# The second layer's experts run between the third and the fourth sequence of attention instead of after it, and the closing gate and residual run inside the fourth sequence's head pairs

## The reference, cut to what matters

```
x  = x + s * g                                  # end of the first layer: "x2"
xn = layernorm(x)
s  = attention(xn)     # 16 heads of 64, rotary, causal, 1024 x 1024 per sequence, output projection Wo: "y"
g  = silu(moe(xn))     # 8 experts, each token goes to 2 of them, weighted; moe(xn) is the sum "z"
x  = x + s * g         # the result
```

## Time and profile before

| | us |
|---|---|
| median of 3 runs | 2559.09 (2556.2 to 2560.73) |
| the profiled execution | 2560.09, its span 2557.7 |
| attention, first to last matmul | 825.6 to 2109.8 |
| experts, first to last matmul | 2115.0 to 2515.0 |
| closing run | 2515.0 to 2557.7 |

### The profile page before, as it was taken

One profiled execution on the slowest core, in us unless ns is written; L12 is line 12 of the kernel. 1 busy time (PEld: TensorE's weight loads), 2 busy tenths in 40 slices (PEclk: granted clock), 3 DMA queues, 4 the chain that ended last, 5 costly groups with the idle time before them and its releaser, 6 DMA issues. The chain is left out here.

```text
span 2557.7 us, 45455 instructions
## 1 busy us (share of the span) xinstructions
PE 2421.2 (95%) x14584; PEld 1698.3 (66%) x14585; DVE 1328.0 (52%) x3699; ACT 1104.5 (43%) x2581; POOL 553.9 (22%) x510
## 2 busy tenths in 40 slices
PE   6999998999976899999999999999999999999993
PEld 5555555666645566666666666666666668999992
DVE  6666341222227866666666666666666653333334
ACT  3211111111115566666666666666666652222222
POOL 3002001444436233332111111111111101111113
PEclk9999998999988999999999999999999999999997
DMA  6013103975446233332111221112221217667696
GB/s 211 17 49 115 49 17 107 271 212 160 115 98 218 77 97 91 97 94 74 42 41 41 52 64 39 35 41 58 67 58 43 58 44 254 236 238 242 236 342 225
DMA packets 145366, 295.74 MB, mean 116 GB/s; under 512 B 16768, under 2 KB 102288, under 8 KB 134896
## 3 DMA queue, kind: packets, MB, share of 16 engines
q1 hardware_dynamic: 124320, 251.59, 31.1%
q0 software_dynamic: 20944, 42.94, 6.3%
HBM read 193.80 MB, written 67.12 MB: 102 GB/s over the span
## 5 line engine op out<-in xcount | busy, mean ns | idle before, releaser
L1463 ACT ACTIVATE at_p<-at_p,at_nmax 128x640 f32<-128x640 f32 (+7 forms) x512 | 392.6, 768 | 179.5 <-DVE at_nmax L1635 173.5
L1498 POOL TENSOR_TENSOR kept_big<-kept_xg 128x1024 f32<-128x1024 f32 x64 | 150.9, 2357 | 985.0 <-DVE kept_xg L1655 985.0
L1470 ACT ACTIVATE at_pT<-at_ps 128x512 f32<-128x512 f32 (+1 forms) x640 | 311.4, 574 | 104.8 <-PE at_ps L1418 104.8
L1635 DVE CUSTOM_DVE_ANT_0 at_p<-at_ps,atk_mask 128x512 f32<-128x512 f32 (+3 forms) x512 | 281.8, 585 | 138.2 <-PE at_ps L1410 134.9
L1418 PEld LDWEIGHTS at_ps<-kept_ident,at_p 128*128 128x128 f32 x2304 | 256.8, 141 | 106.5 <-issue 62.6
L1418 PE MATMUL at_ps<-kept_ident,at_p 128*128 128x128 f32 x2304 | 302.8, 277 | 7.0 <-ACT at_p L1463 6.4
L1410 PE MATMUL at_ps<-kept_big 64*128 64x512 f32 (+3 forms) x1536 | 296.9, 505 | 5.8 <-POOL kept_big L1498 3.3
L1432 PE MATMUL at_ps<-at_pT,at_v 128*64 128x256 f32 (+1 forms) x2560 | 270.2, 362 | 1.2 <-issue 1.2
L1670 DVE SCALAR_TENSOR_TENSOR kept_big<-at_ps,at_inv,kept_big 128x256 f32<-128x256 f32 x512 | 214.0, 475 | 82.0 <-issue 61.5
L1432 PEld LDWEIGHTS at_ps<-at_pT,at_v 128*64 128x64 f32 x2560 | 173.5, 137 | 115.1 <-issue 34.8
L1395 PE MATMUL at_ps<-atk_h,atk_w 128*128 128x512 f32 x512 | 238.0, 598 | 6.6 <-SPq L1257 6.6
(11 more groups left out here) (236 smaller groups left out, 3347.2 us busy)
## 6 DMA issues: line engine op xcount, KB each, us to landing
moe_w<-in_w_w SPq DMA_DIRECT2D x53, 1028.0 KB
kept_xg<-kept_xg SPq DMA_DIRECT2D x256, 128.0 KB
atk_first_w<-in_w_w SPq DMA_DIRECT2D x18, 1028.0 KB
atk_w<-in_w_qkv SPq DMA_DIRECT2D x32, 384.0 KB, 3.1
slot_in<-kept_big SPq DMA_DIRECT2D x9, 1032.0 KB
kept_big<-in_w_eg SPq DMA_DIRECT2D x16, 512.0 KB
kept_big<-in_w_eu SPq DMA_DIRECT2D x16, 512.0 KB
kept_big<-in_w_ed SPq DMA_DIRECT2D x16, 512.0 KB
```

The source lines that it names most:

```text
L1463: act.activation(buf, buf, ACT.Exp, bias=nmax[:, unit:unit + 1], scale=-1.0, accum_out=rsum[:, unit:unit + 1]).then_inc(exp_done, 1)
L1470: act.activation(dst, ring[RING_BANK[part][ev]][:, 0:(i1 - i0) * P].rearrange("p (k c) -> p k c", c=P), ACT.Copy).then_inc(t_read, 1)
L1498: pool.tensor_tensor(out=qkT[x][:, :].rearrange("p (m t) -> p m t", m=2)[:, :, half * CH:(half + 1) * CH], in0=raw[half][:, :].rearrange(" ...
L1635: ins = dve.tensor_tensor_reduce(out=p[unit % LAG][:, at:to], in0=ring[RING_BANK[part]["S", ((t, c), e), ahead]][:, 0:to - at], in1=mask[: ...
```

## The change

`attention` is called twice: for sequences 0 to 2 with the routing and the scatter (`scatter` true), then `moe`, then for sequence 3 alone with `scatter` false. The first call loads, in its last pairs, the projection weights, output weights and normalized input that sequence 3 starts with, and stores sequence 2's y from SBUF at its end. `moe` ends with its last tile; its output rows, their indices and their semaphores now belong to a scope that outlives it.

The closing run is cut into eight groups of 512 tokens and one is worked on in each pair of sequence 3, in the memory of the experts' second weights (`close`, two sets of four buffers of 128x1024). In pair g: SyncE loads both z tables, x2 and y of group g (no y for groups 6 and 7, which are sequence 3 itself), between the output weights and the swaps; GpSimd adds the two z (`begin`); ScalarE takes Exp of minus that, ahead of E6.0; GpSimd adds 1 (`plus`); VectorE takes the reciprocal, ahead of W2.0; in the next pair GpSimd multiplies (`finish`: z times the reciprocal is Silu of z; times y; plus x2), and SyncE stores. For groups 6 and 7 GpSimd makes only the gate, and VectorE multiplies y by it and adds x2 in the last pair, behind the adds of each W. In place of the one Silu there are Exp, plus one, reciprocal and a multiply.

```diff
+CLOSE_EXP, CLOSE_INVERT = ("E", (6, 0), 0), ("W", (2, 0), 0)
...
+        WHOLE = NCH - NCH // B
+        close = [[d.moe_w2[:, (4 * q + k) * TC * C:(4 * q + k + 1) * TC * C] for k in range(4)] for q in range(2)]
...
-                def pair(it, u, load_w, load_wo, half_free=lambda half: None):
+                def pair(it, u, load_w, load_wo, half_free=lambda half: None, then=lambda: None):
                     sp.wait_ge(w_ps, it * 4 + ONE)
                     sp.dma_start(wo[1 - u][:, :], load_wo).then_inc(wo_in[1 - u], 16)
+                    then()
                     for half in range(2):
                         swap(it + 1, half)
...
+                def close_load(g):
+                    q = g % 2
+                    if g >= 2:
+                        sp.wait_ge(close_out[q], 16 * (g // 2) + ONE)
+                    for k in range(TOP):
+                        sp.dma_start(view(close[q][k], g), piece_rows(d.z2, g, k)).then_inc(close_in[q], 16)
+                    sp.dma_start(view(close[q][2], g), piece_rows(d.x2, g)).then_inc(close_in[q], 16)
+                    if g < WHOLE:
+                        sp.dma_start(close[q][3], piece_rows(d.y, g)).then_inc(close_in[q], 16)
...
+                    sp.wait_ge(w_added, nb * (16 * PAIRS) + 16 + ONE)
+                    sp.dma_start(d.y[(nb - 1) * T:nb * T, :].rearrange("(t p) c -> p t c", p=P), tiles(y[:, :], TB)).then_inc(d.y_kept, 16)
+                else:
+                    for u in range(2):
+                        sp.wait_ge(d.moe_scattered[u], 16 * ((FULL_TILES + 1 - u) // 2))
+                    sp.wait_ge(d.y_kept, 16 + ONE)
+                    for pr in range(PAIRS - 1):
+                        load_w = d.w["qkv"][(pr + 3) * P:(pr + 4) * P, :] if pr + 3 < PAIRS else None
+                        pair(pr, pr % 2, load_w, wo_of(pr + 1), then=lambda: close_load(pr))
+                        close_store(pr - 1)
+                    sp.wait_ge(w_ps, (PAIRS - 1) * 4 + ONE)
+                    close_load(PAIRS - 1)
...
+                        if not scatter and part != "first" and ev == CLOSE_EXP:
+                            act.wait_ge(summed, it + 1 + ONE)
+                            act.activation(close[u][1], close[u][0], ACT.Exp, scale=-1.0).then_inc(neg_exp, 1)
...
+                def begin(g):
+                    pool.wait_ge(close_in[g % 2], loaded(g) + ONE)
+                    z0, z1 = close[g % 2][0:2]
+                    pool.tensor_tensor(out=z0, in0=z0, in1=z1, op=ALU.add).then_inc(summed, 1)
+
+                def plus(g):
+                    pool.wait_ge(neg_exp, g + 1 + ONE)
+                    pool.tensor_scalar(close[g % 2][1], close[g % 2][1], 1.0, None, ALU.add).then_inc(plus_one, 1)
+
+                def finish(g):
+                    z0, z1, xa, ya = close[g % 2]
+                    pool.wait_ge(inverted, g + 1 + ONE)
+                    if g >= WHOLE:
+                        pool.tensor_tensor(out=z0, in0=z0, in1=z1, op=ALU.mult).then_inc(gate_ready, 1)
+                    else:
+                        st.done(pool.tensor_tensor(out=z0, in0=z0, in1=z1, op=ALU.mult))
+                        st.wait()
+                        st.done(pool.tensor_tensor(out=z0, in0=z0, in1=ya, op=ALU.mult))
+                        st.wait()
+                        pool.tensor_tensor(out=xa, in0=z0, in1=xa, op=ALU.add).then_inc(closed, 1)
...
+                    rotate(0, 0)
+                    rotate(0, 1)
+                    for pr in range(PAIRS):
+                        if pr > 0:
+                            finish(pr - 1)
+                        begin(pr)
+                        if pr + 1 < PAIRS:
+                            rotate(pr + 1, 0)
+                        plus(pr)
+                        if pr + 1 < PAIRS:
+                            rotate(pr + 1, 1)
+                    finish(PAIRS - 1)
...
+                        if not scatter and part != "first" and ev == CLOSE_INVERT:
+                            dve.wait_ge(plus_one, it + 1 + ONE)
+                            dve.reciprocal(close[u][1], close[u][1]).then_inc(inverted, 1)
...
+                            if e == 1 and part == "last" and not scatter:
+                                z0, xa = (close[n // 2][k][:, n % 2 * 2 * C:(n % 2 + 1) * 2 * C] for k in (0, 2))
+                                part_y = y[:, 2 * n * C:(2 * n + 2) * C]
+                                dve.wait_ge(gate_ready, n // 2 + 1 + ONE)
...
+                                dve.tensor_tensor(out=part_y, in0=part_y, in1=z0, op=ALU.mult).then_inc(gated, 1)
+                                dve.wait_ge(gated, n + 1 + ONE)
+                                dve.tensor_tensor(out=xa, in0=part_y, in1=xa, op=ALU.add).then_inc(out_done, 1)
...
-                attention(nc, d, "at", 0, B, True)
+                attention(nc, d, "at", 0, B - 1, True)
                 moe(nc, d)
+                attention(nc, d, "at2", B - 1, 1, False)
```

More of the change, by code:

```diff
@@ L1239, in run @@
             it = (nb - 1) * PAIRS
-            with eng.Fori(0, PAIRS // 2 - 1) as i:
+            if nb == 1:
+                for u in range(2):
+                    act_on("both", u, u, u, 0)
+            with eng.Fori(int(nb == 1), PAIRS // 2 - 1) as i:
                 for u in range(2):
@@ L1333, in _ @@
[L1333 to L1340, removed]
@@ L1365, in free @@
                         pe.wait_ge(s_read, of * PIECES_NO + PIECES_OF.index((*n[0], n[1])) + 1 + ONE)
-                    else:
+                    elif scatter:
                         pe.wait_ge(counts_read, 1 + ONE)
@@ L1420, in act_on @@
                             last.then_inc(t_ps, 1)
-                        elif kind == "R":
+                        elif kind == "R" and scatter:
                             pe.wait_ge(masks, 1 + ONE)
@@ new lines, in _ @@
+                if scatter:
+                    load_rows(0)
+                    load_rows(1)
+                    pool.wait_ge(numbered, 16 + ONE)
+                    for of in range(nb * PAIRS):
+                        rotate(of, 0)
+                        j = of - 1
+                        if 0 <= j < TOP * B:
+                            if j == 0:
+                                pool.wait_ge(routed, 1 + ONE)
+                            else:
+                                pool.wait_ge(sent, 16 * TB * j)
+                                if j + 1 < TOP * B:
+                                    load_rows(j + 1)
+                            at = j // B * NT + j % B * TB
+                            pool.tensor_copy(row_parts(j)[:, :, C], d.tok_w[:, at:at + TB])
+                            pool.tensor_copy(row_parts(j)[:, :, C + 1], number[:, at:at + TB]).then_inc(marked, 1)
+                            pool.wait_ge(marked, j + 1 + ONE)
+                            pool.wait_ge(rows_in[j % 2], 16 * (j // 2 + 1))
+                            send(j, range(0, TB // 2))
+                        rotate(of, 1)
+                        if of > 0 and of % PAIRS == 0:
+                            end(of // PAIRS - 1)
+                        if 0 <= j < TOP * B:
+                            send(j, range(TB // 2, TB))
+                    pool.wait_ge(sent, 16 * TOP * NT)
+                else:
+                    st = Steps(pool, psteps)
+                    rotate(0, 0)
[10 more added lines that the diff above has]
+                    finish(PAIRS - 1)
@@ L1542, in _ @@
             @block.vector
             def _(dve):
+                if not scatter:
+                    dve.wait_ge(d.y_kept, 16 + ONE)
                 dve.memset(y[:, :], 0.0).then_inc(y_zero, 1)
@@ L1686, in moe @@
         DEEP = 4
-        PIECES = [(g * TC, TC) for g in range(NCH - 1)] + [(NT - TC + t, TC // 2) for t in range(0, TC, TC // 2)]
         b2 = s.sb("b2", E1 * C)
@@ L1787, in _ @@
                                             in_=yo[u][:, :], in_offset=None).then_inc(scattered[u], 16)
-                for g in range(len(PIECES)):
-                    pool.wait_ge(z_in[g], 16 * TOP + ONE)
-                    pool.tensor_tensor(out=z_part(g, 0), in0=z_part(g, 0), in1=z_part(g, 1), op=ALU.add).then_inc(summed, 1)
             @block.tensor
@@ L1857, in _ @@
                 run(act, step)
-                for g in range(len(PIECES)):
-                    act.wait_ge(summed, g + 1 + ONE)
-                    if g >= 4:
-                        act.wait_ge(out_done, g - 4 + 1 + ONE)
-                    act.activation(gate_part(g), z_part(g), ACT.Silu).then_inc(squashed, 1)
             @block.vector
```

149 lines of the change are left out of this document (60 added, 89 removed).

## The result

The changed kernel takes 2585.76 us (median of 4 runs, 2585.36 to 2586.98) beside 2558.73 (2556.2 to 2560.73) for the kernel before: ratio 1.0105, 95% interval 1.0092 to 1.0118. It is 1.05% **slower**; 2597 was forecast, with 2572 to 2620 as the range. All runs of each kernel agree within 0.4%, but for one of experiment 4 (6521.23 us at a granted clock of 0.449), which its ratio leaves out. The profiled execution took 2586.98 us, its span is 2585.2, 27.5 more than before.

A forecast was written before the change was run, and what follows sets the result against it. TensorE was taken to bound the kernel. From 2560.09 us, −45.8 removed and +35.7 added gave 2550; the reciprocal's stalls (+30) and clock drops (+17.5) made 2597.5, say 2597 us, 1.5% slower; range 2572 to 2620.

The forecast's parts named there:

- What bounds it: Whole kernel: TensorE busy 95% of the span; work under attention's matmuls is free unless TensorE is made to wait.
- The reciprocal's length: VectorE's 128x1024 reciprocal in each pair: 6.8 us, from 6.5 ns a column between the 4- and 32-column rows.
- The stall: Ends of pairs 0 to 6: the reciprocal ahead of W2.0 delays A0+ by 4.3 us each, +30 us in all.
- The bound of 2.5 us: Ahead of W2.0: reciprocal time that costs nothing, 2.0 us of VectorE idle time plus 0.5 us of slack.
- The clock: After each of seven stalls TensorE's clock drops, slowing the first two projections by 2.5 us: +17.5 us.
- The first rival: TensorE's clock holds through the stalls or drops in only a few: 2580 us; chance 0.22.
- The gap: Between the experts' last matmul and the fourth sequence's attention: 2.2 plus 2.7 us, together +5.0 us.
- Start, end, experts, store: Refilling attention's pipeline +21 us; new kernel end +10; experts' tiles without closing loads −3.1; y's store before the experts +1.
- a dearer reciprocal: Reciprocal in the pairs costs 8.7 ns a column, 9 us, stall 6.5 us: 2612 us; chance 0.13.
- GpSimd late: GpSimd's closing operations delay the next pair's rotation by up to 4 us and the scores behind it: 2620; chance 0.05.
- Faster: Reciprocal streams at 1.2 us, so no stall and no clock drop in the pairs: 2550 us; chance 0.07.
- the prediction's third rival: GpSimd late in the pairs, some 2620 us, chance 0.05; SBUF contention with VectorE's rotation multiplies changes a few us at most.

The follow-up runs named there:

- experiment 4: Changed kernel with closing runs 0 to 5 left out (loads, stores and operations replaced by their signals): 2556.89 us, ratio 0.9991.
- experiment 1: Changed kernel with VectorE's reciprocal replaced by a multiplication by 1.0 over the same tile, in the same place: 2550.43 us, ratio 0.9968.
- experiment 3: Changed kernel with the reciprocal cut into four instructions of 256 columns, put where VectorE is idle: 2550.86 us, ratio 0.9967.
- experiment 5: Changed kernel with the whole reciprocal ahead of P2+ instead of W2.0, except in the last pair: 2550.07 us, ratio 0.9965.
- experiment 6: Changed kernel with the reciprocal in two halves of 512 columns, one ahead of P2+, one ahead of W2.0 (both there in the last pair): 2556.99 us.
- experiment 2: Changed kernel with the reciprocal issued twice in each pair, once into a tile nobody reads: 2638.34 us.
- experiment 7: Kernel with the reciprocal in quarters, GpSimd's scatters of the last two of 71 expert tiles left out: 2542.15 us.
- experiment 8: Kernel with the reciprocal in quarters, no GpSimd instruction in the experts' block; SyncE stores each tile's rows to a fixed place: 2544.82 us.
- experiment 9: Kernel with the whole reciprocal ahead of P2+, the last two scatters issued at the start of the second attention's block: 2542.69 us, ratio 0.9943.

## Why the prediction was right, and where it was off

**What bounds it**: right. Without a stall the pairs are TensorE's to the hundredth (39.35, experiments 1, 3, 4 and 5). The loads, the Exp and GpSimd's passes, which the prediction put at nothing, cost nothing, and neither does the reciprocal of pair 7.

**The reciprocal's length**: forecast 6.8, measured 6.54. The slope between two rows of 4 and 32 columns carried over a factor of 32: with 256, 512 and 1024 columns (experiments 3 and 6 and the kernel after) the rows are 1.73, 3.34 and 6.54 us, some 6.25 ns a column with 0.13 us of fixed cost. The Trainium skill, "VectorE: DVE Perf Modes", section "Walkthrough: the 8-slice pipeline in each mode", gives the repeat count of 8 from which the prediction worked out an estimate of 8.5 us (8.3 ns a column). The rows are a quarter below that, and the measurement decides.

**The stall**: forecast 4.3, measured 4.06; the difference is the instruction's length (−0.26). The bound of 2.5 us was 2.4 (experiment 6). That the stall arises at A0+ through the ring of banks was right in the main: the transposes T0.0 and T1.0 already wait for the same adds, and A0+ follows them. The last pair, which has no A0+ and A1+, is held for the same 4.0 us up to the end of its first transposes (6.51 us behind S2.0 instead of 2.47 in experiment 1). So the seven stalls are 28.4 us of the 30 forecast.

**The clock**: the direction right, the size wrong; this is the term that was mis-sized most. It was put at 2.5 us a drop, +17.5. Measured: 1.0 in six pairs, and 2.3 in the last one (the rest of its 6.3; S4.0 to S5.0 alone took 3.40 us for 2.21), 8.3 in all. And 2.5 us of such a drop were already in the kernel before: its last pair, 38.03 us, is 35.51 where the clock holds (experiment 1). So stall and clock are 28.4 + 8.3 − 2.5, about 34, instead of 47.5. The step took the cost from two projections that ran at the lower level for 4.9 of their 6.1 us (kernel before, busy time by stretches), as if the level would last that long here:

```profile
825.60:830.53 4.93, 4.93 (x6) 2.13 (x7) 4.69 (x10) 0.60 (x1) 1.81 (x2) 0.50 0.66 204
```

Here it was low for 3.4 us, nearly half of them before A0+, and was back before the two projections ended. With the reciprocal twice the two projections took 1.4 us more than at full speed (experiment 2). The first rival (the clock holds, 2580) had the wrong reason, since the clock did fall, but its time is nearer to the 2585.8 measured than the forecast's 2597: the drops cost little.

**The gap**: wrong, 11.0 instead of 5.0. The step was "the last scatter is issued 2.2 after the last matmul's end", plus the 2.7 of another block's end. It took the end of GpSimd's last counted instruction for the moment at which the barrier can open. Between them lies the drain, 5.9 us, which no view counts; in the kernel before it stands at 2544.76 to 2552.51, hidden behind the last stores, and so could have been found. 2.20 (to the end of the last scatter) + 5.86 + 2.97 = 11.03. What its removal gives is shown by experiments 7 to 9.

**Start, end, experts, store**: +18.2 for +21 (nearer still to the 19 that the first attention would give without its routing), +10.5 for +10, −2.8 for −3.1, −0.1 for +1. The store of y is hidden in the time between the blocks.

**The rivals**: a dearer reciprocal (2612) is out by the row; GpSimd late (2620) too: its rotation began 24.5 us into the pair instead of 19.4, and it stood idle for 11 us before that, waiting for VectorE's product.

```profile
2379.88 2.36 POOL L1570 TENSOR_TENSOR kept_big<-kept_xg 128x1024 f32<-128x1024 f32 x1 [10.98 <-DVE kept_xg L1767]
```

Faster (2550 if the reciprocal is under 2.5 us): it didn't occur, but experiment 1 shows that the mechanism was right, and its time is 2550.4. That the two agree so well is partly luck, since the gap (+6.0) was made up for by the start (−2.8), the store (−1.1) and the last pair, where the clock held (−2.5).

## What to carry to other kernels

Work laid under another engine's matmuls is free by its place, not by the average: look in the in-order queue for what stands behind the new instruction and how soon it is needed, and put a long one ahead of what is needed latest. Here the same 6.5 us cost 5 ahead of the adds that free PSUM banks, and nothing ahead of a rotation whose result is wanted in the next pair. And before a stage is moved away from the end of a kernel, look at what the end had hidden: drains and barriers cost nothing behind the last stores, and all they take in the middle.

## What the runs showed of the hardware

- A reciprocal on VectorE is 6.25 ns a column of float32, over nine times the multiplication by a constant over the same tile (6.54 and 0.68 us for 1024 columns).
- GpSimd's drain after 69 to 71 indirect scatters lasts 5.7 to 5.9 us beyond its last instruction. Waiting for the transfers doesn't explain it: in the kernel before the last scatter had ended 27.5 us before the drain began, and from the end of GpSimd's last addition (2541.83 + 4.80, row below) the drain lasted 5.9 us all the same. The Trainium skill, "Perfetto Trace Analysis", section "DMA Instruction — SWDGE (GPSIMD)", says that the profiler's end of such a DMA is when its descriptors are made, not when the data has moved; this trace agrees, with 0.97 us a scatter and a median of 2.5 us from issue to landing, but by that the last one lands some 4 us before the drain ends. After the first attention's block, whose GpSimd had made 64 scatters and waited for them itself, it was 2.1 us beyond the last instruction (1754.75 + 2.35 to 1759.24), with two scatters in a block (experiment 9) 0.24, with none 0.07. The experts' 71, 69 and two scatters (5.86, 5.70, 0.24) lie near 0.08 us each, but the 64 of the first attention don't, nor do the first layer's two blocks (16 indirect DMAs and 2.5 us, 112 and 6.9). What the drain does in that time, and what it grows with, stays open.
- 2 MB of loads, five passes of GpSimd and an Exp per pair left the pair at 39.35 us (experiments 3 and 4). Whether GpSimd slows VectorE's products with two inputs in SBUF, as the prediction's third rival considered, isn't shown: none of the 32 rotation products of the second attention overlapped an operation of GpSimd.
- The same 2.12 us of wait in the last pair was followed by the lower clock in the kernel before and not in experiment 1; the drop cost 2.5 us.

GpSimd's last additions in the kernel before (timeline):

```profile
2541.83 4.80 POOL L1790 TENSOR_TENSOR moe_w<-moe_w,kept_big 128x1024 f32<-128x1024 f32 x3 [0.66 <-DMA kept_big<-z_rows]
```
